# One batch of one-hots on ScalarE, other zero products and joined marks in a graph-attention kernel

## The reference, cut to what matters

```python
HW = h @ W
s = HW @ a[:512, 0];  t = HW @ a[512:, 0]
e = leaky_relu(s[row] + t[col], 0.2)            # row = src, col = dst
att = softmax of e over the edges of each row
agg = segment_sum(att[:, None] * h[col], row)
out = silu(agg) @ base_w.T + einsum('nip,oip->no', b_splines(agg), spline_w)
x = layernorm(x + out)
```

## Time and profile before

| | |
|---|---|
| median of 3 runs | 394.05 us (393.69 to 394.08) |
| the profiled execution | 394.55 us, span 392.7 us |
| TensorE busy | 378.9 us (96%) |
| VectorE busy | 343.8 us (88%) |
| ScalarE busy | 251.6 us (64%) |
| GpSimd busy | 35.3 us (9%) |
| the batches of counts | about 5 to 47 us |
| row blocks | about 47 to 141 us |
| spline layer and norm | about 141 to 390 us |

### The profile page before, as it was taken

One profiled execution on the slowest core, in us unless ns is written; L12 is line 12 of the kernel. 1 busy time (PEld: TensorE's weight loads), 2 busy tenths in 40 slices (PEclk: granted clock), 3 DMA queues, 4 the chain that ended last, 5 costly groups with the idle time before them and its releaser, 6 DMA issues.

```text
span 392.7 us, 5016 instructions
## 1 busy us (share of the span) xinstructions
PE 378.9 (96%) x1878; PEld 299.2 (76%) x1878; DVE 343.8 (88%) x430; ACT 251.6 (64%) x241; POOL 35.3 (9%) x88
## 2 busy tenths in 40 slices
PE   5999979899999999999999999999999999999994
PEld 2546648788888888778888888888888888888883
DVE  8999989986777498999899999889999899999345
ACT  1669944434445879865886766777758686866222
POOL 5001210000000001011010101001010101001000
PEclk9999989999999999999999999999999999999998
DMA  7900990000000036549546455723423454733202
GB/s 255 389 15 6 189 278 6 3 0 0 2 0 2 0 111 213 159 130 310 175 120 186 125 164 157 204 65 86 128 58 104 129 166 134 226 90 88 76 27 101
DMA packets 23482, 45.90 MB, mean 117 GB/s; under 512 B 1862, under 2 KB 2074, under 8 KB 23458
## 3 DMA queue, kind: packets, MB, share of 16 engines
q0 software_dynamic: 12400, 24.00, 24.0%
q1 hardware_dynamic: 11058, 21.58, 17.1%
HBM read 43.02 MB, written 2.56 MB: 116 GB/s over the span
## 4 chain that ended last, share of the span: by engine, by line
PE 80%; DVE 14%; issue 3%; POOL 1%; ACT 1%; DVEq 0%; POOLq 0%; ACTq 0%
PE PS L1240 63%; PE PS L1183 14%; DVE oh L435 5%; DVE still L449 3%; PE PS L1164 2%; DVE ex L625 1%; PE PS L1193 1%; DVE pl L735 1%; DVE ex L715 0%; DVE scrap L691 0%; DVE scrap L609 0%; ACT ph L927 0%; ACT ex L920 0%; DVE st L814 0%; DVE xr L809 0%
## 5 line engine op out<-in xcount | busy, mean ns | idle before, releaser
L1240 PE MATMUL PS<-wh,s 128*128 128x512 f32 x720 | 223.1, 390 | 0.0
L1240 PEld LDWEIGHTS PS<-wh,s 128*128 128x128 f32 x720 | 135.1, 188 | 29.6 <-issue 1.5
L1240 PE MATMUL PS<-wl,s 128*128 128x512 f32 x360 | 140.1, 389 | 0.0
L1240 PEld LDWEIGHTS PS<-wl,s 128*128 128x128 f32 x360 | 67.6, 188 | 13.7
L976 ACT ACTIVATE s<-v 128x1280 fp32r<-128x1280 f32 (+1 forms) x32 | 40.0, 1251 | 40.7 <-DVE v L792 24.6
L959 ACT ACTIVATE v<-xt,bias 128x1280 f32<-128x1280 f32 (+1 forms) x32 | 42.9, 1341 | 19.6 <-DVE s L802 17.6
L786 DVE SCALAR_TENSOR_TENSOR v<-v,v 128x1280 f32<-128x1280 f32 (+1 forms) x32 | 46.4, 1451 | 6.3 <-ACT v L962 6.3
L792 DVE SCALAR_TENSOR_TENSOR v<-v,v 128x1280 f32<-128x1280 f32 (+1 forms) x32 | 46.8, 1461 | 3.3
L802 DVE SCALAR_TENSOR_TENSOR s<-v,s 128x1280 fp32r<-128x1280 f32 (+1 forms) x32 | 46.5, 1455 | 3.4 <-ACT s L976 3.4
L426 POOL DMA_DIRECT2D wh<-in_splT x32 | 22.9, 715 | 271.8 <-PE PS L1240 184.2
L788 DVE SCALAR_TENSOR_TENSOR v<-v,v 128x1280 f32<-128x1280 f32 (+1 forms) x32 | 46.5, 1454 | 0.0
(11 more groups left out here) (141 smaller groups left out, 333.5 us busy)
## 6 DMA issues: line engine op xcount, KB each, us to landing
wh<-in_splT POOLq DMA_DIRECT2D x32, 512.0 KB, 4.2
wring<-in_splT SPq DMA_DIRECT2D x21, 512.0 KB, 4.0
xt<-in_xT SPq DMA_DIRECT2D x1, 2500.0 KB, 12.3
xh<-in_x POOLq DMA_DIRECT2D x1, 2304.0 KB, 11.8
out<-xr SPq DMA_DIRECT2D x9, 256.0 KB
wh<-in_baseT POOLq DMA_DIRECT2D x4, 512.0 KB, 5.9
xl<-in_x POOLq DMA_DIRECT2D x1, 1536.0 KB, 13.1
wring<-in_baseT SPq DMA_DIRECT2D x3, 512.0 KB, 4.7
```

The costliest lines, as they stand in the source:

```text
L1240: m = e.matmul(PS[:, w % 8, :], sx[:, ic, tl * 128:tl * 128 + 128], wx[:, ic, :], start=first and n == 0, stop=last and n == 2)
```

## The change

- The moving one-hots of batch 3 (`BY_SCALAR`) are made by ScalarE: a copy of the 64 places, then twice four `Abs` of the distance (one for each tile) and one `Relu` of 1 minus it over four tiles. TensorE waits for `s_by` there.
- The x load's tenth block has its last rows zeroed by GpSimd (a memset of the whole block, ahead of the load), so that products and the negation use 128 rows instead of 98.
- A product of zeros clears bank 6 ahead of `st_rows`, and one copy of 66 partitions takes the place of three. The sign of `s_part` is turned, and with it two operations that read it.
- `s_column` stands after batch 12 instead of 13, `t_spread` after 14, 15 and 17 instead of 15, 15 and 16.
- One product of zeros in each batch from 11 to 18, in place of two in 14 to 16. Behind the loop 16, 5 and 2 instead of 8, 6 and 2.
- Behind the loop one mark of windows 20 to 24 for blocks 0 and 1, once all counts are there; the later mark takes windows 20 to 24 of blocks 2 to 9 (before, windows 20 and 21 of all ten blocks were marked ahead).
- `back(j - 1)` stands ahead of `sums(j, 2)`.

The diff, without most of its context:

```diff
@@ -23,6 +23,7 @@
 RB = 4
+BY_SCALAR = 3
 MID, PER_TILE, PER_BATCH = 45, 75, 602
@@ -70,7 +71,7 @@
 SETUP = {n: k + 1 for k, n in enumerate(
-    ["im", "mid", "tile", "nought", "id0", "ident", "xpad", "bigb", "wpad", "half", "eps", "down", "up"]
+    ["im", "mid", "tile", "nought", "id0", "ident", "rest", "xpad", "bigb", "wpad", "half", "eps", "down", "up"]
     + [f"bias{p}" for p in range(2 * NP + 1)] + ["lplace", "limits"])}
@@ -91,6 +92,8 @@
         mk = sb("mk", [128, NCP, 2], F16)
+        mk_by = sb("mk_by", [128, TB])
+        off = sb("off", [128, TB // 2, 2 * REACH[BY_SCALAR]], F16)
...
@@ -141,7 +144,7 @@
         still = at("still", 27, [128, RB, TB, 128], BF16)
-        nought = at("nought", 28, [128, CW], BF16, 3072)
+        nought = at("nought", 28, [128, HALF], BF16, 3072)
         xl = at("xl", 15, [128, NT, F], F32R)
@@ -212,8 +215,8 @@
-        WA_AT, WT_AT, ST_AT, SC_AT = (0, 1, 2, 3), 5, (7, 8, 9, 10), 13
-        TB_AT = (15, 15, 16)
+        WA_AT, WT_AT, ST_AT, SC_AT = (0, 1, 2, 3), 5, (7, 8, 9, 10), 12
+        TB_AT = (14, 15, 17)
         ENDS_AT, MOST_AT, SIZES_AT = 5, 8, NB - 1
@@ -221,9 +224,9 @@
-        MARKED, MARKED_AHEAD, NEAR = 20, 22, 2
-        WARM_AT = range(14, NB - 4)
+        MARKED, NEAR = 20, 2
         LOADS_AT = SIZES_AT - 2
+        WARM_AT = range(11, NB - 2)
         TABLE = 19
@@ -376,6 +379,7 @@
                             pattern=[[-1, 128]], channel_multiplier=1).then_inc(s_setup, 1)
+            e.memset(xh[:, NT - 1, :].bitcast(F32), 0.0).then_inc(s_setup, 1)
             e.memset(xt0[:, :, N:RP], 0.0).then_inc(s_setup, 1)
@@ -402,6 +406,7 @@
             e.wait_ge(s_w, 32)
+            e.wait_ge(s_setup, SETUP["rest"])
             e.dma_start(xh[:, 0:NT - 1, :], x[0:1152, :].rearrange("(w p) i -> p w i", p=128)).then_inc(s_xh, 16)
@@ -429,6 +434,8 @@
+                if b == BY_SCALAR:
+                    return
                 h = REACH[b]
@@ -623,7 +630,7 @@
                 return e.scalar_tensor_tensor(out=ex[:, j % 3, lo:hi], in0=gentle[:, lo:hi], scalar=s_part[:, j:j + 1],
-                                              in1=trow[:, lo:hi], op0=ALU.subtract, op1=ALU.max)
+                                              in1=trow[:, lo:hi], op0=ALU.add, op1=ALU.max)
@@ -649,12 +656,9 @@
                     greatest_of(0, slice(0, DW * MARKED), LW).then_inc(s_early, 1)
-                    e.wait_ge(s_cnt, taken(MARKED_AHEAD - 1))
-                    marks(MARKED, MARKED_AHEAD).then_inc(s_ahead, 1)
                     e.wait_ge(s_cnt, len(TAKEN))
-                    marks(MARKED_AHEAD, ND, 0, NEAR).then_inc(s_near, 1)
+                    marks(MARKED, ND, 0, NEAR).then_inc(s_near, 1)
                     e.wait_ge(s_early, n + 1)
-                    e.wait_ge(s_ahead, n + 1)
                     e.wait_ge(s_ovp, n + 1)
@@ -699,7 +703,7 @@
                                        ).then_inc(s_small, 1)
-                e.scalar_tensor_tensor(out=y, in0=t, scalar=-SLOPE, in1=s8, op0=ALU.mult, op1=ALU.add
+                e.scalar_tensor_tensor(out=y, in0=t, scalar=-SLOPE, in1=s8, op0=ALU.mult, op1=ALU.subtract
                                        ).then_inc(s_small, 1)
@@ -747,7 +751,7 @@
             weigh(1)
-            marks(MARKED_AHEAD, ND, NEAR, NT).then_inc(s_marked, 1)
+            marks(MARKED, ND, NEAR, NT).then_inc(s_marked, 1)
             e.wait_ge(s_marked, 1)
@@ -861,10 +865,30 @@
+            def moving_by_scalar():
+                h, b = REACH[BY_SCALAR], BY_SCALAR
+                k = TB // 2
+                e.wait_ge(s_setup, SETUP["im"])
+                e.wait_ge(s_mk, 1)
+                e.copy(mk_by[:, :], mk[:, TB * b:TB * b + TB, 0]).then_inc(s_by_mk, 1)
+                e.wait_ge(s_by_mk, 1)
+                for part in range(2):
+                    if part:
+                        e.wait_ge(s_by, part)
+                    for t in range(k):
+                        m = e.activation(off[:, t, :], im[:, MV // 2 - h:MV // 2 + h], ACT.Abs,
+                                         bias=mk_by[:, part * k + t:part * k + t + 1], scale=-1.0)
+                    m.then_inc(s_off, 1)
+                    e.wait_ge(s_off, part + 1)
+                    e.activation(oh[:, b % RB, part * k:part * k + k, 0:2 * h], off[:, :, :], ACT.Relu, bias=1.0,
+                                 scale=-1.0).then_inc(s_by, 1)
+            moving_by_scalar()
             def st_rows():
                 e.wait_ge(s_sr, 1)
-                for k, (lo, hi) in enumerate(TCH):
-                    e.copy(strow[32 * k:32 * k + 2, 0:hi - lo], PS[32 * k:32 * k + 2, 6, 0:hi - lo]).then_inc(s_srow, 1)
+                e.copy(strow[0:66, :], PS[0:66, 6, :]).then_inc(s_srow, 1)
@@ -896,14 +920,13 @@
                     k = NEGATIVE_AT[b]
-                    r = rows(k)
                     e.wait_ge(s_xh, 32)
-                    e.mul(xl[0:r, k, :], xh[0:r, k, :].bitcast(F32), -1.0).then_inc(s_neg, 1)
+                    e.mul(xl[:, k, :], xh[:, k, :].bitcast(F32), -1.0).then_inc(s_neg, 1)
                 if b == SC_AT:
                         e.mul(s_part[:, lo // 128:hi // 128],
-                              PS[:, 6 + k % 2, lo // 64:hi // 64].rearrange("p (j a) -> p j a", a=2)[:, :, 0], 1 - SLOPE
+                              PS[:, 6 + k % 2, lo // 64:hi // 64].rearrange("p (j a) -> p j a", a=2)[:, :, 0], SLOPE - 1
                               ).then_inc(s_scol, 1)
@@ -1065,6 +1088,7 @@
                     e.wait_ge(s_setup, SETUP["xpad"])
+                    e.matmul(PS[:, 6, :], nought[:, 0:128], nought[:, :], start=True, stop=True)
                 for k, (lo, hi) in enumerate(TCH):
@@ -1073,7 +1097,7 @@
-                e.wait_ge(s_srow, 3)
+                e.wait_ge(s_srow, 1)
                 e.wait_ge(s_tab, 11)
@@ -1098,19 +1122,21 @@
-                e.matmul(PS[:, w % 6, 0:CW], nought[:, 0:128], nought[:, :], start=True, stop=False)
-            def keep_warm(n, bank=6, start=True):
+                e.matmul(PS[:, w % 6, 0:CW], nought[:, 0:128], nought[:, 0:CW], start=True, stop=False)
+            def keep_warm(n):
                 for k in range(n):
-                    e.matmul(PS[:, bank, 0:CW], nought[:, 0:128], nought[:, :], start=start, stop=start)
+                    e.matmul(PS[:, 6, 0:CW], nought[:, 0:128], nought[:, 0:CW], start=True, stop=True)
             for b in range(NB):
-                e.wait_ge(s_mv, b + 1)
+                if b == BY_SCALAR:
+                    e.wait_ge(s_by, 2)
+                else:
+                    e.wait_ge(s_mv, b + (b < BY_SCALAR))
                 e.wait_ge(s_head, b + 1)
@@ -1122,7 +1148,7 @@
                 if b in WARM_AT:
-                    keep_warm(2, w % 6, start=False)
+                    e.matmul(PS[:, w % 6, 0:CW], nought[:, 0:128], nought[:, 0:CW], start=False, stop=False)
                 if b in WA_AT:
@@ -1179,8 +1205,7 @@
                 for t in range(a, b):
-                    r = rows(t)
-                    m = e.matmul(PS[:, 5 + j % 2, :], pp[0:r, j % 3, place(j, t), :], xs[0:r, t, :],
+                    m = e.matmul(PS[:, 5 + j % 2, :], pp[:, j % 3, place(j, t), :], xs[:, t, :],
                                  start=(i == 0 and t == 0), stop=(i == end and t == NT - 1))
@@ -1194,9 +1219,9 @@
             e.wait_ge(s_trow, 3)
-            keep_warm(8)
+            keep_warm(16)
             e.wait_ge(s_tmax, 1)
-            keep_warm(6)
+            keep_warm(5)
             e.wait_ge(s_ex, 1)
@@ -1213,8 +1238,8 @@
                     turn(j + 1)
+                back(j - 1)
                 sums(j, 2)
-                back(j - 1)
                 e.wait_ge(s_shi, u + 1)
```

8 lines of the change are left out of this document (4 added, 4 removed).

## The result

The changed kernel takes **395.32 us** (median of 9 runs, 393.82 to 395.83) against 394.05 (393.69 to 394.57, 9 runs): a ratio of 1.0022, interval 1.0012 to 1.0031, slower by 0.22%. I had forecast 393.7. Its times are spread over 2 us, those of before over 0.9. That one was in its turn among the longer ones of before, whose times lie in two groups, near 394.05 and near 394.55 us. So the two traces side by side hide the loss.

The account below looks back on a forecast made before the run. VectorE was taken to bound the kernel to 71.7 us, with TensorE almost as full in the loop, then TensorE. Terms -0.67 + 0.05 + 0.22 = -0.40 on 394.05 gave 393.65, forecast 393.7 us, range 392.6 to 395.5.

Parts of the forecast that it names:

- What bounds the kernel: Whole kernel: VectorE's chain from 5 to 71.7 us, TensorE's from 74.35; in the one-hot loop both are almost full.
- The level: Whole time: -0.40 us put on the median of 394.05 us gives 393.65, forecast as 393.7 us.
- Part 1: One-hot loop, fourth batch: moving one-hots to ScalarE save VectorE 1.18 us; ScalarE's added 5.3 us cost 0.
- the cover of 0.9 us: ScalarE, start of the loop: time left between its added one-hot work, ending at 10.7 us, and the first evacuation.
- Part 2: TensorE in the loop: 0.94 idle + 0.10 moved t piece - 0.63 added products, last batch 0.41 us earlier.
- Part 4: Marks behind the loop: merged near mark starts at 48.09 us, 0.67 earlier; larger marks cost 0.05 and 0.22 us.
- the term of -0.67: Near mark behind the loop: starts as the counts come, at 48.09 instead of 48.76 us.
- -0.26 + 0.05 + 0.22: Joining the marks behind the loop: 0.26 us saved, 0.05 and 0.22 us added by larger marks, about 0 together.
- Part 5: Behind the loop: more zero products keep the clock up at 52 us, wait before `sums(2,0)` 1.6 us; `back` moved; worth 0.
- B: Loop's end: VectorE's saving comes through, -1.17 us, 392.9 us; chance 0.22.
- C: TensorE at 72 us: clock falls after a 1.6 us wait before `sums(2,0)`, costing 1.7 us, 395.4 us; chance 0.15.
- D: Loop: nothing arrives, ScalarE late or zero products dearer than 0.21 us each; 394.1 to 394.5 us; chance 0.12.

Follow-up runs that it names:

- early_start: a_again with four more products of zeros ahead of the first batch (the steady base): 393.34 us (393.26 to 393.51).
- a_again: The changed kernel with the short loop's waits on constants instead of registers, no other edit: 394.11 us (393.46 to 396.0).
- b_early: The kernel before, with constant waits as in b_again, plus four products of zeros at the start: 394.08 us (394.06 to 394.57).
- e_vector: early_start with the fourth batch's moving one-hots back on VectorE: 396.49 us (394.93 to 396.57).
- e_warm0: early_start without the eight products of zeros in batches 11 to 18: 392.02 us (392.0 to 392.06).
- e_keep: early_start with 8, 6 and 2 products of zeros behind the loop instead of 16, 5 and 2: 393.45 us (393.31 to 393.53).
- b_again: The kernel before with the short loop's waits on constants instead of registers, no other edit: 394.11 us (394.01 to 394.6).
- fill72: a_again with seven products of zeros in TensorE's wait before `sums(2, 0)`: 394.25 us (393.88 to 395.57).
- x_late: a_again with GpSimd's memset of the tenth block moved to just ahead of the x load: 394.73 us (393.82 to 395.6).
- marks_plain: a_again with the marks behind the loop as before the change: 394.67 us (393.88 to 396.31).

## Why the prediction was wrong, point by point

**What bounds the kernel.** "Two engines in step: taking work from one alone moves the end by no more than the slack of the other" was right, and the changed kernel is that sentence. What I didn't draw from it is that the bound then lies on TensorE from 8 us on, and with it whatever delays TensorE there: the time until its clock rises and the landing of `a`. I had only looked for the clock at waits of the steady state, and "TensorE falls behind VectorE in batches 1 to 7 anyway" stood in the sum as a cover, at no cost. This step failed: early_start against a_again differs in nothing else and takes away 0.8 us of median and 2.3 us of spread.

**The level, a second step that failed.** I read -0.40 us from a trace of 394.55 us and put it on the median of 394.05. The trace was of before's upper group, where VectorE starts 0.51 us late; the median's group doesn't have these 0.51 us to give. In b_early's trace the near mark starts at 48.26 us. My forecast of 48.09 is only 0.17 us ahead of that, less than the 0.27 that the larger marks were to cost, so the same sum gives about 0.1 us more than 394.05, not 393.65.

**Part 1.** VectorE's saving was right (1.18 of 1.96 us) and incomplete: 0.27 us more come from its earlier start through the memset, which I had at 0 with 0.5 as an upper bound of cost; that it could be a gain was missing. The last 0.51 us are a gain only against the upper group of before, to which the trace belongs. ScalarE's side, timeline of the changed kernel:

```profile
4.74 0.20 ACT L874 CAST mk_by<-mk 128x8 f32<-128x8 f16 x1 [0.45 <-DVE mk L493]
4.97 1.74 ACT L880 ACTIVATE off<-im,mk_by 128x268 f16<-128x268 f16 x4
6.75 1.10 ACT L884 ACTIVATE oh<-off 128x1072 bf16<-128x1072 f16 x1
...
9.65 1.10 ACT L884 ACTIVATE oh<-off 128x1072 bf16<-128x1072 f16 x1
10.80 0.99 ACT L898 CAST C<-PS 128x1000 uint16<-128x1000 f32 x1
```

An Abs costs 0.435 us (1.74 / 4), not 0.3; the whole 6.0 us, not 5.3. The first evacuation follows with no idle, so the cover of 0.9 us is used up to the last, and nothing waited for it. "I take 0" held, and e_vector shows the gain of the step on the steady base: the last product 1.17 us earlier.

**Part 2, the step that failed in size.** Forecast 0.94 + 0.10 - 0.63 = 0.41 us earlier; measured 0.03 later at the end of the last product, in spite of VectorE's 0.78 us more; 0.54 later than in b_early's trace. The term "another 0.10 us goes because the third piece of t is moved" read one row and overlooked the next: the x4 of 40.05 us was two pieces at once, and taking them apart costs 1.05 us of TensorE (1.15 in the traces, 1.16 in the median). The 0.10 us itself was misread: a product of t starts 0.30 instead of 0.21 us after a zero product wherever the two follow each other (36.89 to 37.19), so it was no wait for the copy of the first piece and moving the third piece doesn't save it. The added products were priced rightly at 0.21 us and up, but e_warm0 shows that all eight, not only the three added, stood on the path.

**Part 4.** Near mark forecast at 48.09, came at 48.51: the term of -0.67 became -0.25, since it hung on the last product. The merge itself, -0.26 + 0.05 + 0.22, measured +0.24 on the steady base: its -0.26 needs VectorE to be late, and it no longer is.

**Part 5.** The clock at 52 us, the wait of 0.15 us before `tmax`'s products, and 1.71 us before `sums(2, 0)` (forecast 1.6) came as said, and e_keep confirms the value 0. But this was in part luck: b_again has the full clock at 52 us and a wait of 1.67 us with the old eight products, and e_keep has no half clock either after a wait of 1.86 us. `back` ahead of `sums(j, 2)` I gave 0; it is worth 0.3 to 0.4 us, so "nothing that the change touches" behind 74.35 us was wrong too.

**Rivals.** B (VectorE's saving comes through) fell. C fell: at 1.71 us of wait no fall in the changed kernel's trace, none by the mean granted clock in its other executions, nor anything to gain in fill72; its mechanism is real (1.99 us, e_vector). D named the right place, TensorE, with the right price of a zero product, but as "the last batch starts as before or 0.4 us later", without the late clock that, as argued below, makes 394.3 into 395.5.

**The medians.** The changed kernel lies at 395.32, a_again at 394.11. The stop of 0.46 us, which a_again doesn't have, accounts for about 0.4 of the 1.2 us. The rest would be more executions with a late start of TensorE; the profiled execution of the changed kernel was not one of them, so this part is argued from x_late and marks_plain, not shown. About 0.8 of the 1.27 us by which the changed kernel is slower rest on it. The two kernels also weren't measured side by side, and whether the chip or the waits on registers have a share wasn't tried.

## What to carry to other kernels

Before work is moved off the bounding engine, list what the next engine has hidden so far, its first microseconds included: a slow start that cost nothing becomes a cost one for one, and shows first as spread. When a row of small products is moved, look at how many ran in its duration; apart, they may cost as often as there are pieces. When savings on two engines have been measured singly, measure them together before adding them. Before a sum read from a trace is put on a median, look whether the traced execution lies where the median lies; if the times come in groups, a trace of each is needed.

## What the runs showed of the hardware that I had not expected

- TensorE's first products ran at half speed until some moment between 10 and 13 us (without early products), another one in traces of kernels with the same start; four products of zeros at 5 us made the first batch run at 1.06 instead of 1.49 us and narrowed the times from 2.5 to 0.25 us.
- The same wait (TensorE for `ph`) was followed by no fall of the clock at 1.02 and 1.71 us and by one at 1.99 us; the wait for `tmax` by one at 2.02 us (before) and by none at 2.05 us (b_again). The length of a wait alone doesn't decide it.
- Two pairs of products with two rows each, in partitions 0 and 32, took together what one pair takes: 1.06 and 1.05 us.
- A VectorE operation of 128x176 took 0.25 to 0.78 us at the start, beside GpSimd's setup operations. Edges that arrived 0.15 us later made VectorE's first one-hot 0.51 us later (b_early, before).
- A stop of TensorE of 0.46 us without a visible cause, in the third unit of the spline layer of three kernels, and in none of the others.
